# Gated hidden values kept in DRAM by tiles of tokens, one of their loads behind the keys and queries, and the last turn of maxima four slots later

## The chip, the cores and the metric

The kernel runs on one core of a Trainium2 chip. The metric is the device time of one execution in microseconds (us); the time before is the median of three runs.

## The reference, cut to what matters

`x` is [2, 1024, 512] in float32, that is 2048 tokens. The layer normalises it and feeds it to a causal attention with 32 heads of 16 (8 groups of keys and values, each for 4 heads) and to a gated feed-forward net; the input is added at the end.

```python
xn = layernorm(x)
q = (xn @ Wq)                      # 32 heads of 16
k, v = (xn @ Wkv)                  # 8 groups, each for 4 heads
w = softmax(where(causal, -inf, q @ k.T) / 4)
s = (w @ v) @ Wo + bo
gate = xn @ gate_w.T + (xn @ gate_a.T) @ gate_b.T
up = xn @ up_w.T + (xn @ up_a.T) @ up_b.T
hidden = silu(gate) * up           # [2048 tokens, 1376]
y = hidden @ down_w.T + (hidden @ down_a.T) @ down_b.T
out = x + s * silu(y)
```

## The kernel before

**Precision.** Matrix products of float32 values are done on high and low parts: three products (high by high, high by low, low by high) stand for one. So the gated values `hidden` exist twice, as `hid_hi` and `hid_lo`.

**Stages.** Tokens come in 4 chunks of 512 (`NCH`, `C`) or 16 tiles of 128 (`NT`, `P`), and the 1376 hidden values in 11 blocks `h` of at most 128 (`NH`). After some 100 us of normalising and projecting, two streams of work run side by side on every engine. The *attention* goes through 16 groups (`N`, 8 groups of 2 sequences) in rounds of 40 slots (`SLOTS`). The *background* first makes the gated values (`hidden(h, c)`, 44 pieces), then folds the down weights (`fold_down(h)`, 11 pieces), then does the down product of 16 tiles of tokens (`down(t)`) with the output product (`output(t)`) one tile behind, or four behind for the last tiles. `interleave` decides when background steps come between two slots; it counts steps and knows no times.

**The gated values in DRAM.** All 1376 hidden values of a tile are needed for its down product, but they are made block by block. So `store_hidden` writes each piece to the scratch tensor `hid`, laid out as [2 parts, 11 blocks, 128 rows, 2048 tokens]: a row of a piece is 512 tokens, 2048 bytes in one run. `load_hidden(t)` reads the 2 x 11 x 128 rows of a tile back, 128 tokens of each, 512 bytes in one run (2816 runs, 1408 KB), into one of two buffers `hin`, which the down product reads. Block 10 has only 96 rows, so SP writes zeros to its last 32 rows of `hid` at the start. Loads 0 and 1 stand in the order of SP behind the fold of block 5, load t + 2 behind the down product of tile t.

**SP issues every DMA**, in one order and on one hardware queue. Its attention part issues, for the group to come, keys and queries (`L867`, `L870`, slot 1 of a round) and values (`L878`, slot 19), and the attention output and its sums (`L894`, `L898`, `L902`). If SP waits, everything behind it waits too.

**Maxima.** The softmax needs the maximum of each row ahead. For each group TensorE (PE) makes the scores once in bank `s` (`L1146`) for VectorE (DVE) to take maxima (`L1723`, `L1726`); `split_max` (`L1733` to `L1739`) puts them into `neg_pad`. Then comes a *turn*: PE transposes `neg_pad` (`L1153`), ScalarE (ACT) copies it to `neg_rows` (`L1450`), and SP copies it in four small DMAs into two rows of `q` (`L886`), so that the second score product (`st`, `L1165`) has the maximum in it. That product runs a group behind the first one; the exponentials (`L1442`) and the product with the values (`o`, `L1182`) follow. Each group has two turns, one for each half of its rows. The second must have landed at slot 12 of the group's own round.

**What sets the place of a turn.** `STREAM` lists score units and turns; `stream_slots` gives each a slot. The second turn of a group stands behind the first pair of units of the next group, which is slot 6 of its own round. The very last turn has no next group: it stands in the slot of the last pair of units, slot 2 of round 15. Before a turn PE waits in `turn_max` for `m_split`, the end of `split_max`.

Of the kernel before, what the change touches and what calls it, by code (L numbers as in the profile page):

```python
# [6 lines left out]
F32 = mybir.dt.float32  # L7
# [6 lines left out]
P = 128  # L14
C = 512
# [3 lines left out]
B, T, D, F, R = 2, 1024, 512, 1376, 16  # L19
H, G = 32, 8  # L20
HD, REP = D // H, H // G
TOK = B * T
KT = D // P
NCH, TT = TOK // C, C // P
NT = TOK // P
NH = -(-F // P)
rows = [min(P, F - P * h) for h in range(NH)]
FULL = F // P
NBLK = H * HD // P + 1
N = B * G  # L30
QT = T // P
ROWS = 3 * HD
AUG = ROWS + 2
# [47 lines left out]

LOAD, LOAD_V = 1, 19
FIRST_UNIT, UNIT_SLOTS = 6, 39
FIRST_OF_ALL = 10

EVEN_SLOTS = range(22, 31)
# [54 lines left out]
def out_behind(t):  # L141


    if t >= NT - TT:
        return t - TT
    return t - 1 if 1 <= t <= NT // 2 else None
# [110 lines left out]
def stream_slots():  # L257

    weight = [150 + spec[2] for _, _, spec in UNIT]
    slots, slot = [], -1
    for kind, n in STREAM:
        if kind == "unit" and n % 2 == 0:
            g, w = divmod(n, NU)
            first = FIRST_UNIT if g else FIRST_OF_ALL
            even = SLOTS * g + first + (UNIT_SLOTS + FIRST_UNIT - first) * sum(weight[:w]) // sum(weight)
            even -= even % 2
            slot = max(even, slot + 1)
            if slot - SLOTS * g in EVEN_SLOTS:  # L270
                slot += slot % 2
        slots.append(slot)
    return slots


STREAM_SLOT = stream_slots()


# [11 lines left out]

def layer(nc, x, Wq, Wkv, Wo, bo, gate_w, up_w, down_w, low_a, low_b, low_a_down, low_b_down, out):
    scratch = dict(
        q=[B, H, AUG, T], k=[G, B, 3, HD, T], v=[G, B, P, QT, HD], hid=[2, NH, P, TOK],
        o=[B, 2, 2 * HD, H, C], r=[B, 2, H, C],
    )
    s = {n: nc.dram_tensor(f"scratch_{n}", shape, F32).ap() for n, shape in scratch.items()}
    with ExitStack() as ctx:

        def sbuf(stack, name, shape, dt=F32):
            return stack.enter_context(nc.sbuf_tensor(name, shape, dt))  # L300

        def in_place(stack, name, shape, part):


            with ExitStack() as brief:
                whole = sbuf(brief, name, shape)
            return whole, sbuf(stack, name + part, shape, F32R)
# [5 lines left out]
        q = sbuf(ctx, "q", [P, 2, 2, T], F32R)  # L313
        k = sbuf(ctx, "k", [P, 2, T], F32R)
        v = sbuf(ctx, "v", [P, 3, QT, 2, HD])
# [17 lines left out]
        with ExitStack() as first:  # L333
# [15 lines left out]
            with ExitStack() as own:  # L349
# [5 lines left out]
                hid, hid_l = in_place(own, "hid", [P, 2, C], "_lo")  # L355


        zeros = prob[:, 0, 0]
# [7 lines left out]
        with ExitStack() as second:  # L366
# [7 lines left out]
            late, hin = in_place(second, "late_context", [P, 2, 2, NH, P], "_hid_in")  # L374
# [116 lines left out]
        def wait_filled(engine, key):  # L491
            engine.wait_ge(filled, NUMBER[key] + 1)
# [49 lines left out]
        def _(pool):  # L542
# [44 lines left out]
            def low_context(t):  # L587
                pool.wait_ge(ch_done, CONTEXT_COUNT[t])
                _, whole, _, hi, lo = context_place(t)
                pool.tensor_tensor(lo, whole, hi, ALU.subtract).then_inc(cl_done, 1)  # L590
# [67 lines left out]
        def _(sp):  # L658
# [60 lines left out]
            def load_more_raw(n):  # L719
                if n + 8 < RAWS:  # L720
                    load_raw(n + 8)

            def store_hidden(n):
                h, c = divmod(n, NCH)
                sp.wait_ge(hid_lo, n + 1)
                for j, part_ in enumerate((hid_h, hid_l)):
                    sp.dma_start(s["hid"][j, h, 0:rows[h], c * C:(c + 1) * C], part_[0:rows[h], n % 2].bitcast(F32))\
                        .then_inc(hid_stored[n % 2], DMA)

            def load_hidden(t):  # L730
                if t >= 2:
                    wait_filled(sp, ("down", t - 2, 0))
                else:
                    sp.wait_ge(zero_stored, (B + 2) * DMA)
                    for i in range(2):
                        sp.wait_ge(hid_stored[i], 2 * DMA * NH * NCH // 2)
                sp.dma_start(hin[:, t % 2].rearrange("p j h n -> p (j h) n").bitcast(F32),
                             s["hid"][:, :, :, t * P:(t + 1) * P].rearrange("j h p n -> p (j h) n"))\
                    .then_inc(hin_landed[t % 2], DMA)

            def load_out(t):
# [17 lines left out]
            def load_again(t):  # L759
                if t >= 5:  # L760
                    sp.wait_ge(r3_done, t - 4)
                sp.dma_start(xt[:, t % 5], x_tiles[t]).then_inc(x_again[t % 5], DMA)

            def store_out(t):
                sp.wait_ge(r3_done, t + 1)
                sp.dma_start(out_tiles[t], ring[:, t % 8]).then_inc(out_stored[t % 8], DMA)

            def background():
# [41 lines left out]
                for h in range(NH):  # L810
                    yield STEPS["down_fold"]
                    load_more_raw(RAW_DOWN + h)
                    if h == 2:
                        sp.dma_start(wo[:, :, :], Wo.rearrange("(p k) n -> p k n", k=KT)).then_inc(wo_landed, DMA)
                        sp.dma_start(bias[:, :], bo.rearrange("(o n) -> o n", o=1).to_broadcast((P, D)))\
                            .then_inc(wo_landed, DMA)
                    if h == 3:
                        store_hidden(NCH * NH - 1)
                    if h == 5:
                        load_hidden(0)  # L820
                        load_hidden(1)
                yield STEPS["rest"]
                load_out(0)
                load_again(0)
                for t in range(NT):
                    yield LOAD_AT
                    if t + 1 < NT // 2:
                        load_out(t + 1)
                    for ahead in {11: (8,), 12: (9, 10)}.get(t, ()):
                        load_out(ahead)  # L830
                    if t + 1 < NT - 3:
                        load_again(t + 1)
                    yield STEPS["down"] - LOAD_AT
                    if t + 2 < NT:
                        load_hidden(t + 2)
                    if 2 <= t < 2 + NT // 2:
                        store_out(t - 2)
                    if t == NT - 1:
                        load_out(NT - 2)
                    if out_behind(t) is not None:  # L840
                        yield STEPS["out"]
                        for ahead in {12: (11,), 13: (12,), 14: (13, 15)}.get(t, ()):
                            load_out(ahead)
                        if t > NT - TT:
                            store_out(out_behind(t) - 1)
                            load_again(t)
# [70 lines left out]
                sp.dma_start(s["q"][b, :, ROWS:, :].rearrange("h r (a n) -> h (r a) n", n=C), zeros)\  # L917
                    .then_inc(zero_stored, DMA)
            for j in range(2):
                sp.dma_start(s["hid"][j, FULL, rows[-1]:].rearrange("p (a n) -> (p a) n", n=C), zeros)\  # L920
                    .then_inc(zero_stored, DMA)
            sp.wait_ge(const, 4)
            for a in range(2):
# [874 lines left out]
```

## Time and profile before

| | us |
|---|---|
| median of 3 runs | 944.62 |
| the three runs | 943.69, 944.62, 946.37 |
| the profiled execution | 946.66 |
| its span, first to last instruction | 944.9 |

In the span PE is busy for 896.9 us (95%), DVE for 583.7 us, ACT for 488.5 us and GpSimd for 314.7 us. All 142946 packets move 129.20 MB at a mean of 137 GB/s. The mean granted clock of TensorE is 0.984 of full speed (2.4 GHz). A row of a timeline gives start and length in us, engine, line, operation, tiles and count; what stands in brackets at its end is how long the engine had been idle before it, and what released it. SPq is SP's DMA issue; its length is the time that issuing takes, not the transfer.

### The profile page before, as it was taken

Reading aid. Unit: us, or ns where it says so; the run is one execution under the profiler, and the core shown is the slowest. Engines: PE = TensorE matmul, PEld = TensorE weight load, DVE = VectorE, ACT = ScalarE, POOL = GpSimd, SP = SyncE. Lnnn points to the kernel's source line nnn. Section 1 sums busy time; section 2 is a strip of 40 time slices with the busy share of each in tenths; the row PEclk is TensorE's granted clock in tenths of the full one; section 3 lists DMA queues with packets and bytes.
Section 4 is the critical chain, followed back from the end, with each engine's and each line's share of the span. In section 5 each row is a group of like instructions: output and inputs, shape, how many; then the busy total and the mean of one; then the engine's idle time right before and its main releaser. Section 6 shows DMA issues by size and latency. Waiting matters only on the chain.

```text
span 944.9 us, 21107 instructions
## 1 busy us (share of the span) xinstructions
PE 896.9 (95%) x8075; PEld 633.1 (67%) x8075; DVE 583.7 (62%) x1688; ACT 488.5 (52%) x990; POOL 314.7 (33%) x316
## 2 busy tenths in 40 slices
PE   3898999999999999999999999999889999999997
PEld 3765667676766666667676766554667777777885
DVE  7756666666666666665656565777666666650136
ACT  3522656565555656565656565656445454546211
POOL 4231235252525343525252434441121313121133
PEclk9978999999999999999999999998999999999999
DMA  9466343333333342424242434347565647415774
GB/s 290 165 193 192 92 129 97 122 97 114 108 115 110 97 130 83 137 71 148 58 138 84 126 99 121 100 142 204 155 183 156 171 124 194 137 53 171 205 216 142
DMA packets 142946, 129.20 MB, mean 137 GB/s; under 512 B 36176, under 2 KB 104368, under 8 KB 142624
## 3 DMA queue, kind: packets, MB, share of 16 engines
q1 hardware_dynamic: 142848, 127.87, 45.6%
q8 instruction: 65, 1.06, 0.5%
q14 instruction: 33, 0.27, 0.1%
HBM read 74.07 MB, written 53.22 MB: 135 GB/s over the span
## 4 chain that ended last, share of the span: by engine, by line
PE 88%; DVE 5%; DMA 3%; ACT 2%; issue 2%; SPq 1%; DVEq 0%
PE bank L1011 27%; PE o L1182 14%; PE bank L1045 12%; PE s L1146 10%; PE st L1165 8%; PE bank L286 4%; PE bank L287 4%; PE bank L288 4%; DMA ring<-in_L_attn_x 2%; PE bank L986 1%; PE bank L990 1%; DMA q<-scratch_q 1%; DVE junk L1723 1%; PE s L1153 1%; ACT prob L1442 1%
## 5 line engine op out<-in xcount | busy, mean ns | idle before, releaser
L1442 ACT ACTIVATE prob<-st 128x512 f32<-128x512 f32 (+1 forms) x640 | 323.2, 554 | 263.4 <-PE st L1165 262.8
L1723 DVE CUSTOM_DVE_ANT_0 junk<-s,mask 128x128 bf16<-128x128 f32 (+3 forms) x512 | 229.1, 487 | 69.7 <-PE s L1146 67.9
L1726 DVE TENSOR_REDUCE part_max<-s 128x1 f32<-128x512 f32 x256 | 164.0, 682 | 116.3 <-PE s L1146 116.1
L1146 PE MATMUL s<-k,q 64*128 64x512 f32 (+3 forms) x768 | 150.7, 379 | 12.2 <-DVE part_max L1723 4.6
L567 POOL TENSOR_SCALAR_AFFINE_SELECT prob<-prob 128x512 f32<-128x512 f32 x128 | 81.8, 652 | 225.8 <-ACT prob L1442 224.3
L1011 PE MATMUL bank<-x_hi,w_hi 64*128 64x512 f32 (+1 forms) x704 | 150.2, 412 | 2.4 <-DVE hid L1564 1.1
L1182 PE MATMUL o<-prob,v 128*32 128x512 f32 (+3 forms) x1536 | 145.4, 497 | 0.0
L1011 PE MATMUL bank<-x_lo,w_hi 64*128 64x512 f32 (+1 forms) x704 | 142.8, 391 | 0.0
L1011 PE MATMUL bank<-x_hi,w_lo 64*128 64x512 f32 (+1 forms) x704 | 142.1, 389 | 0.0
L1165 PE MATMUL st<-q,k 64*128 64x512 f32 (+3 forms) x768 | 130.7, 356 | 2.3 <-ACT prob L1442 1.8
L1146 PEld LDWEIGHTS s<-k,q 64*128 64x128 f32 x768 | 79.1, 188 | 53.6 <-DVE part_max L1723 24.4
L1045 PE MATMUL bank<-down_hi,late_context_hid_in 64*128 64x256 f32 x1056 | 113.7, 288 | 0.3 <-DVE y L1580 0.3
L576 POOL TENSOR_TENSOR tanh<-tanh,hid 128x512 f32<-128x512 f32 (+1 forms) x44 | 56.6, 1286 | 163.7 <-DVE hid L1564 163.7
L1045 PEld LDWEIGHTS bank<-down_hi,late_context_hid_in 64*128 64x128 f32 x1056 | 91.4, 189 | 17.9 <-issue 16.9
L1011 PEld LDWEIGHTS bank<-x_hi,w_hi 64*128 64x128 f32 (+1 forms) x704 | 69.4, 182 | 40.1 <-issue 30.6
L1165 PEld LDWEIGHTS st<-q,k 64*128 64x128 f32 x768 | 73.5, 186 | 28.5 <-issue 11.0
L1182 PEld LDWEIGHTS o<-prob,v 128*32 128x32 f32 x1536 | 39.7, 110 | 64.0 <-issue 58.1
L584 POOL TENSOR_TENSOR hid_lo<-hid,tanh_hid_hi 128x512 fp32r<-128x512 f32 (+1 forms) x44 | 56.8, 1292 | 71.8 <-ACT tanh_hid_hi L1299 71.8
L1045 PE MATMUL bank<-down_lo,late_context_hid_in 64*128 64x256 f32 x528 | 77.5, 281 | 0.9 <-issue 0.9
L1011 PEld LDWEIGHTS bank<-x_lo,w_hi 64*128 64x128 f32 (+1 forms) x704 | 69.2, 182 | 12.3
L1011 PEld LDWEIGHTS bank<-x_hi,w_lo 64*128 64x128 f32 (+1 forms) x704 | 69.4, 183 | 7.7
L578 POOL TENSOR_TENSOR hid<-tanh,hid 128x512 f32<-128x512 f32 (+1 forms) x44 | 56.7, 1288 | 3.5
(148 smaller groups left out, 1089.0 us busy)
## 6 DMA issues: line engine op xcount, KB each, us to landing
late_context_hid_in<-scratch_hid SPq DMA_DIRECT2D x16, 1408.0 KB, 7.2
q<-scratch_q SPq DMA_DIRECT2D x60, 200.0 KB
scratch_hid<-tanh_hid_hi SPq DMA_DIRECT2D x40, 256.0 KB, 2.1
scratch_hid<-hid_lo SPq DMA_DIRECT2D x40, 256.0 KB, 2.4
scratch_o<-o_sb SPq DMA_DIRECT2D x32, 256.0 KB
scratch_q<-proj_hi SPq DMA_DIRECT2D x30, 256.0 KB
k<-scratch_k SPq DMA_DIRECT2D x30, 192.0 KB
x_again<-in_L_attn_x SPq DMA_DIRECT2D x16, 256.0 KB, 4.4
```

The lines of the kernel that those rows point to most:

```text
L567: ins = pool.affine_select(out=blk, in_=blk, compare_op=ALU.is_ge, fill=0.0, base=0, pattern=[[0, REP], [1, P]], channel_multiplier=-1)
L576: pool.tensor_tensor(th[0:hp, n % 2], th[0:hp, n % 2], hid[0:hp, n % 2], ALU.mult).then_inc(tanh_used, 1)
L578: pool.tensor_tensor(hid[0:hp, n % 2], th[0:hp, n % 2], hid[0:hp, n % 2], ALU.add).then_inc(hid_done, 1)
L584: pool.tensor_tensor(hid_l[0:hp, n % 2], hid[0:hp, n % 2], hid_h[0:hp, n % 2], ALU.subtract)\
L1011: mm = pe.matmul(bank[i][0:hp, :], w_[half, h % 2, i, kt, 0:hp], x_[half, c, kt], start=not cross and kt == 0 and w_ is wh and x_ is xh, s ...
L1045: mm = pe.matmul(bank[i][:, COLUMNS[i]], lhs[half], rhs[half, COLUMNS[i]], start=not cross and n == 0 and m == 0, stop=cross == 1 and n == ...
L1146: pe.matmul(sb_[(p + odd) % S_BANKS][:, 0:wd], q[half, g % 2, h // 2, qt * P:(qt + 1) * P], k[half, g % 2, k0:k0 + wd], start=True, stop=T ...
L1165: mm = pe.matmul(st[odd][:, col:col + q1 - q0], k[half, i % 2, kt * P:(kt + 1) * P], q[half, i % 2, h // 2, q0:q1], start=True, stop=True)
L1182: mm = pe.matmul(ob[32 * h:32 * h + 2 * HD, q0 % C:q0 % C + q1 - q0], v[:, i % 3, kt].rearrange("p a e -> p (a e)"), prob[:, job % 3, h, c ...
L1442: nc.scalar.activation(prob[:, job % 3, h, 0:JOB_COLS[j]], st[at % ST_BANKS][:, 0:JOB_COLS[j]], ACT.Exp, scale=float(HD) ** -0.5).then_inc ...
L1723: ins = dve.tensor_tensor_reduce(junk[:, n % S_BANKS, 0:wd], bank_[:, 0:wd], mask[:, C - wd:C], 1.0, LOWEST, ALU.add, ALU.max, part[:, h, ...
L1726: ins = dve.tensor_reduce(part[:, h, qt, dst:dst + 1], bank_[:, 0:wd], AX.X, ALU.max)
```

## The change

There are four parts.

1. `hid` is laid out as [16 tiles, 128 rows, 2 parts, 11 blocks, 128 tokens]. A load of a tile now reads 128 runs of 11264 bytes, where it read 2816 of 512 bytes. A store of a piece now writes 4 runs of 512 bytes for each row, where it wrote one of 2048 (512 runs for 128). The two zero fills write 512 runs of 512 bytes each, from 128 rows of 2048. The bytes are the same.
2. Load 0 stands behind the fold of block 4, load 1 behind that of block 6.
3. Load 2 stands five steps into `down(1)`, behind the keys and queries of the next group; it stood behind `down(0)`, ahead of them.
4. The last turn is four slots later, in slot 6 of round 15.

```diff
--- before.py
+++ after.py
@@ -81,6 +81,7 @@
 
 LOAD, LOAD_V = 1, 19
 FIRST_UNIT, UNIT_SLOTS = 6, 39
+LAST_TURN = 4
 FIRST_OF_ALL = 10
 
 EVEN_SLOTS = range(22, 31)
@@ -270,6 +271,8 @@
             if slot - SLOTS * g in EVEN_SLOTS:
                 slot += slot % 2
         slots.append(slot)
+
+    slots[-1] += LAST_TURN
     return slots
 
 
@@ -290,7 +293,7 @@
 
 def layer(nc, x, Wq, Wkv, Wo, bo, gate_w, up_w, down_w, low_a, low_b, low_a_down, low_b_down, out):
     scratch = dict(
-        q=[B, H, AUG, T], k=[G, B, 3, HD, T], v=[G, B, P, QT, HD], hid=[2, NH, P, TOK],
+        q=[B, H, AUG, T], k=[G, B, 3, HD, T], v=[G, B, P, QT, HD], hid=[NT, P, 2, NH, P],
         o=[B, 2, 2 * HD, H, C], r=[B, 2, H, C],
     )
     s = {n: nc.dram_tensor(f"scratch_{n}", shape, F32).ap() for n, shape in scratch.items()}
@@ -724,7 +727,8 @@
                 h, c = divmod(n, NCH)
                 sp.wait_ge(hid_lo, n + 1)
                 for j, part_ in enumerate((hid_h, hid_l)):
-                    sp.dma_start(s["hid"][j, h, 0:rows[h], c * C:(c + 1) * C], part_[0:rows[h], n % 2].bitcast(F32))\
+                    sp.dma_start(s["hid"][TT * c:TT * (c + 1), 0:rows[h], j, h].rearrange("t p n -> p t n"),
+                                 part_[0:rows[h], n % 2].bitcast(F32).rearrange("p (t n) -> p t n", t=TT))\
                         .then_inc(hid_stored[n % 2], DMA)
 
             def load_hidden(t):
@@ -734,8 +738,8 @@
                     sp.wait_ge(zero_stored, (B + 2) * DMA)
                     for i in range(2):
                         sp.wait_ge(hid_stored[i], 2 * DMA * NH * NCH // 2)
-                sp.dma_start(hin[:, t % 2].rearrange("p j h n -> p (j h) n").bitcast(F32),
-                             s["hid"][:, :, :, t * P:(t + 1) * P].rearrange("j h p n -> p (j h) n"))\
+                sp.dma_start(hin[:, t % 2].rearrange("p j h n -> p (j h n)").bitcast(F32),
+                             s["hid"][t].rearrange("p j h n -> p (j h n)"))\
                     .then_inc(hin_landed[t % 2], DMA)
 
             def load_out(t):
@@ -816,8 +820,9 @@
                             .then_inc(wo_landed, DMA)
                     if h == 3:
                         store_hidden(NCH * NH - 1)
-                    if h == 5:
+                    if h == 4:
                         load_hidden(0)
+                    if h == 6:
                         load_hidden(1)
                 yield STEPS["rest"]
                 load_out(0)
@@ -830,8 +835,10 @@
                         load_out(ahead)
                     if t + 1 < NT - 3:
                         load_again(t + 1)
+                    if t == 1:
+                        load_hidden(2)
                     yield STEPS["down"] - LOAD_AT
-                    if t + 2 < NT:
+                    if 1 <= t < NT - 2:
                         load_hidden(t + 2)
                     if 2 <= t < 2 + NT // 2:
                         store_out(t - 2)
@@ -917,7 +924,7 @@
                 sp.dma_start(s["q"][b, :, ROWS:, :].rearrange("h r (a n) -> h (r a) n", n=C), zeros)\
                     .then_inc(zero_stored, DMA)
             for j in range(2):
-                sp.dma_start(s["hid"][j, FULL, rows[-1]:].rearrange("p (a n) -> (p a) n", n=C), zeros)\
+                sp.dma_start(s["hid"][:, rows[-1]:, j, FULL], zeros)\
                     .then_inc(zero_stored, DMA)
             sp.wait_ge(const, 4)
             for a in range(2):
```

SP around the start of the down products. L737 of before and L741 of after are the load of a tile of hidden values, L867/L874 and L870/L877 the next keys and queries. Before:

```order
L727 DMA scratch_hid<-hid_lo 96x512
L737 DMA late_context_hid_in<-scratch_hid 128x22x128 x2
L894 DMA scratch_o<-o_sb 4x32x512
...
L762 DMA x_again<-in_L_attn_x 128x512
L737 DMA late_context_hid_in<-scratch_hid 128x22x128
L867 DMA k<-scratch_k 48x1024 x2
L870 DMA q<-scratch_q 50x1024 x4
L754 DMA ctx<-scratch_o 128x4x128
L756 DMA inv_sums<-scratch_r 128x4x128
L762 DMA x_again<-in_L_attn_x 128x512
L894 DMA scratch_o<-o_sb 4x32x512
```

After:

```order
L730 DMA scratch_hid<-hid_lo 96x4x128
L741 DMA late_context_hid_in<-scratch_hid 128x2816
L901 DMA scratch_o<-o_sb 4x32x512
...
L766 DMA x_again<-in_L_attn_x 128x512
L874 DMA k<-scratch_k 48x1024 x2
L877 DMA q<-scratch_q 50x1024 x4
L758 DMA ctx<-scratch_o 128x4x128
L760 DMA inv_sums<-scratch_r 128x4x128
L766 DMA x_again<-in_L_attn_x 128x512
L741 DMA late_context_hid_in<-scratch_hid 128x2816
L901 DMA scratch_o<-o_sb 4x32x512
```

Load 2 went from ahead of the keys and queries to a place five DMAs and more behind them; the second of the first two loads stands two DMAs further back.

PE at the last turn (`neg_pad` to `s`). Before:

```order
L1165 MATMUL st<-q,k 128x512 x2
L1146 MATMUL s<-k,q 128x512 x2
L1153 MATMUL s<-ident,neg_pad 32x128
L1182 MATMUL o<-prob,v 32x256 x4
L1045 MATMUL bank<-wo_hi,ctx_hi 128x256 x2
```

After, four slots on:

```order
L1172 MATMUL st<-q,k 128x384 x2
L1172 MATMUL st<-q,k 128x128 x2
L1160 MATMUL s<-ident,neg_pad 32x128
L1189 MATMUL o<-prob,v 32x512 x4
L1052 MATMUL bank<-down_hi,late_context_hid_in 128x256 x2
```

The turn now stands behind two more second score products of round 15 and an output product; nothing else changed its place on PE.

SP at the same time of the program, before:

```order
L762 DMA x_again<-in_L_attn_x 128x512
L886 DMA q<-neg_rows 2x4x128 x4
L737 DMA late_context_hid_in<-scratch_hid 128x22x128
L766 DMA out<-ring 128x512
L894 DMA scratch_o<-o_sb 4x32x512
L898 DMA sums<-scratch_o 128x16
```

After:

```order
L766 DMA x_again<-in_L_attn_x 128x512
L741 DMA late_context_hid_in<-scratch_hid 128x2816
L770 DMA out<-ring 128x512
L901 DMA scratch_o<-o_sb 4x32x512
L893 DMA q<-neg_rows 2x4x128 x4
L905 DMA sums<-scratch_o 128x16
```

The four small DMAs of the turn now stand behind a hidden load, a store of results and a store of attention output.

## Rows read from the trace of the kernel before

**Rows 1.** Page, part 1: busy us (share of the span) x instructions.
```profile
PE 896.9 (95%) x8075; PEld 633.1 (67%) x8075; DVE 583.7 (62%) x1688; ACT 488.5 (52%) x990; POOL 314.7 (33%) x316
```
**Rows 2.** Busy us (x instructions) of PE, PEld, DVE, ACT, POOL; clock; DMA share; GB/s.
```profile
100.00:600.00 500.00, 498.32 (x4258) 336.44 (x4256) 319.74 (x984) 294.72 (x604) 207.49 (x205) 1.00 0.36 109
```
**Rows 3.** What PE waited for in 640 to 945: us, times, longest.
```profile
PE s L1146 <- DMA q<-scratch_q: 2.1, 1, 2.1
PE s L1153 <- DVE neg_pad L1739: 2.0, 1, 2.0
```
**Rows 4.** Timeline of SP, from load 2 to the turn behind it.
```profile
680.72 0.38 SPq L737 DMA_DIRECT2D late_context_hid_in<-scratch_hid  x1
681.21 3.50 SPq L867 DMA_DIRECT2D k<-scratch_k  x2
684.75 1.48 SPq L870 DMA_DIRECT2D q<-scratch_q  x4
...
694.06 2.64 SPq L886 DMA_DIRECT2D q<-neg_rows  x4
```
**Rows 5.** Timeline of PE across the wait for the queries.
```profile
690.34 0.50 PE L1165 MATMUL st<-q,k 64*128 64x384 f32 x4
692.93 0.47 PE L1146 MATMUL s<-k,q 64*128 64x128 f32 x2 [2.08 <-DMA q<-scratch_q]
...
697.52 0.28 PE L1165 MATMUL st<-q,k 64*128 64x256 f32 x2
```
**Rows 6.** Windows for PE behind both long waits: busy, clock, DMA share, GB/s.
```profile
693.00:694.00 1.00, 1.00 (x7) 0.50 0.64 156
...
843.00:844.00 1.00, 0.46 (x6) 1.00 0.00 0
```
**Rows 7.** Timeline of PE, the same stretch of the next round.
```profile
744.55 0.27 PE L1146 MATMUL s<-k,q 64*128 64x128 f32 x2
...
747.61 0.28 PE L1165 MATMUL st<-q,k 64*128 64x256 f32 x2
```
**Rows 8.** Timeline of SP, keys and queries of that next round.
```profile
734.32 0.81 SPq L867 DMA_DIRECT2D k<-scratch_k  x2
735.17 1.48 SPq L870 DMA_DIRECT2D q<-scratch_q  x4
```
**Rows 9.** Timeline of PE, last turn to slot 12 of round 15.
```profile
843.54 0.28 PE L1153 MATMUL s<-ident,neg_pad 128*32 128x128 f32 x1 [2.04 <-DVE neg_pad L1739]
...
847.92 1.06 PE L1182 MATMUL o<-prob,v 128*32 128x512 f32 x8
...
853.19 0.43 PE L1165 MATMUL st<-q,k 64*128 64x512 f32 x2
```
**Rows 10.** Timeline of SP at the last turn.
```profile
844.15 2.58 SPq L886 DMA_DIRECT2D q<-neg_rows  x4
```
**Rows 11.** A turn in the hidden stage: SP, then PE's slot 12.
```profile
587.78 2.68 SPq L886 DMA_DIRECT2D q<-neg_rows  x4
...
593.30 0.42 PE L1165 MATMUL st<-q,k 64*128 64x512 f32 x2
```
**Rows 12.** What SP waited for in 110 to 600.
```profile
SPq L886 <- ACT neg_rows L1450: 90.2, 20, 6.8
```
**Rows 13.** Small DMA of 8 KB (tile sums), issue to landing.
```profile
DMA to landing us min/median/max: 1.5/2.1/7.2
```
**Rows 14.** Windows for PE: runs of 2 KB and more; runs of 512 bytes.
```profile
8.00:12.00 4.00, 0.00 (x0) 1.00 1.06 384
...
660.00:664.00 4.00, 3.01 (x27) 1.00 1.15 342
```
**Rows 15.** Chain in order of time: the load of x at the start.
```profile
16.11 9.91 DMA ring<-in_L_attn_x
```
**Rows 16.** Timeline of SP: behind 1024 runs of 512 bytes, and behind few.
```profile
726.67 1.41 SPq L762 DMA_DIRECT2D x_again<-in_L_attn_x  x1
...
826.26 0.43 SPq L762 DMA_DIRECT2D x_again<-in_L_attn_x  x1
```

## Prediction, made before the changed kernel ran

> **What bounds the kernel now.** The page's busy times come first: PE is busy for 896.9 of 944.9 us, every other engine for 62% or less [rows 1]. Nothing is won by making another engine faster; what counts is where PE stands still or runs at half clock. The stretches say where: from 100 to 600 PE is busy for 498.32 of 500 us at full clock [rows 2], so the ten rounds of hidden values have 1.7 us to give in all, and only something that makes PE wait can change them. What is lost lies at the start and behind 600. There the list of PE's waits names two long ones that single places cause: 2.1 us for the queries and 2.0 us for `neg_pad` [rows 3]. The timelines of PE and SP at these two places carry the rest.
>
> The sum goes against the profiled execution, 946.66 us. That is 2.04 us above the median of 944.62; I take the difference to be spread that the change leaves alone, and take the same sum off the median.
>
> **Load 2 behind the keys and queries.** SP issues the load of a hidden tile at 680.72 in 0.38 us, and then needs 3.50 us for the two key DMAs, which took 0.81 us one round later [rows 4, 8]. So the issue itself was held for 2.7 us, with 2816 runs of the load still outstanding. The queries come out at 684.75 instead of about 682, and their data stand behind the load in the same queue. PE needs them at 690.84 and gets them at 692.93: 2.08 us idle [rows 5]. In the next round, with no load just ahead, the keys are issued at 734.32 and PE uses them at 744.55 with no wait, 10.2 us later [rows 7, 8]. In the changed kernel the keys come out at 681.2 (SP waits there for a score product that is done by then), 9.6 us before 690.84. What must move in front of them is gone: the load took 1408 KB, at 297 GB/s (below) 4.9 us of the queue, plus the 2.7 us of held issue. Together 7.6 us earlier against 2.08 us of wait leaves 5.5 us to spare. This term is **-2.08**.
>
> The clock goes with it. Behind the gap the granted clock falls to 0.50, that is from 2.4 to 1.2 GHz [rows 6]. From the first score of that slot to the second score product of slot 8 PE takes 697.52 - 692.93 = 4.59 us; the same work one round later takes 747.61 - 744.55 = 3.06 us [rows 5, 7]. The half clock costs 1.53 us. PE was dense before the gap, so without the gap I expect no fall: **-1.53**. The bounds are 0 (the fall comes anyway) and -1.53.
>
> What is late next: load 2 itself is not, since it comes out at about 685.5 and `down(2)` starts a whole tile later. The turn behind it (at 694.06 [rows 4]) moves up by the gap too, to about 691.8 to 694.4, and its data stand behind queries, context and load 2. Slot 12 of that round is then near 699: 690.84 plus 8.2 us (the 9.8 us it takes now less 1.53). A turn's last DMA may be late there by 0 to 0.5 us; I take 0, because the whole queue has nearly drained by 697 in the trace of before with the same bytes.
>
> **The last turn.** PE waits 2.04 us for the end of `split_max` [rows 9]. Four slots later, at 847.92 - 2.04 = 845.9, `neg_pad` is long done: **-2.04**, with no clock to win, as the clock stayed at 1.00 there [rows 6]. But the turn has a reader: slot 12, at 853.19 - 2.04 = 851.15 [rows 9]. PE's turn ends at 846.15, the copy by ACT behind an exponential at 846.8, SP issues four DMAs in about 2.6 us [rows 10] to 849.5. The smallest DMAs take 2.1 us from issue to landing [rows 13], of which 0.46 is issue, so the last lands at about 851.1. From the other side: in the hidden stage the issue ends at 590.46 and PE goes on at 593.30 without a wait [rows 11], so 2.84 us are surely enough, which would be 852.35. The new wait is between 0 (that median, empty queue) and 1.2 us; I take **+0.5**, nearer to the small DMA's own duration. On SP the four DMAs now stand behind hidden load, result store and output store. These three can go out from 841.1, when their waits are met, and 1.9 MB take under 6 us, so the queue is empty before 849; if it is not, each us of backlog is a us at slot 12.
>
> **The layout, loads.** Rows of 11264 bytes instead of 512. With long rows (x, weights, mostly 2 KB and more) the queue moved 384 GB/s at a share of 1.06, that is 362 at full share; with rows of 512 bytes 342 at 1.15, that is 297 [rows 14]. A load of 1408 KB thus needs 4.0 us of the queue instead of 4.9, and with 128 runs instead of 2816 SP should no longer be held for about 3 us behind each of 16 loads. PE waits for none of the other loads or for what follows them (no other DMA is among its waits), so this is **0**, with cover by PE's own work. Bounds 0 and about -0.5, if the wait of a later stage hangs on it by a chain I don't see.
>
> **The layout, stores.** 88 stores write four times the runs. At 297 instead of 362 GB/s each takes 0.16 us longer; the DMA share in that stage is 0.36 [rows 2], and the buffer is used again two pieces (20 us) later. **0** as long as SP keeps its slack: see the third rival. The zero fills are another matter. They stand ahead of the third load of x at the start, and the chain goes through that load for 9.91 us [rows 15] at a full queue. Half a MB costs 1.77 us at 297 and 1.45 at 362: **+0.3**, bounds 0 and 0.6.
>
> By the Trainium skill (DMA: Bandwidth & Descriptors, the table at its head) 512 bytes are already enough for line rate. Then the zero fills would cost nothing and the sum would be -5.2 instead of -4.9; the two windows above speak for a fifth less, though what else ran in them differs.
>
> **The first two loads.** SP waits at load 0 until the last store of hidden values has landed, before and after, so moving it up one block changes nothing; load 1 behind two small DMAs leaves room for them. PE's waits from 655 to 680 are for DVE and ACT. **0**.
>
> **Sum:** -2.08 - 1.53 - 2.04 + 0.5 + 0.3 = **-4.85 us**: 941.8 against the profiled execution, **939.8** against the median.
>
> **Rivals.**
>
> *The gain is half of that (941.3 to 943.0).* The turn's landing takes the place of one of the two waits: +1.2 at slot 12 of round 15, or a like wait in the first round of down products, or the clock falls in spite of the gap being gone. For it: the path at round 15 has no spare time at all in my own working, and the half clock hangs on one gap of 2.08 us, while one of 2.04 us at 841.5 left the clock at 1.00 [rows 6]. Against it: other turns never make PE wait. With one of these the sum is -3.3, with all three -1.6.
>
> *Ten engines.* By the Trainium skill (DMA: Bandwidth & Descriptors, why a DMA increments its semaphore by 16) a DMA whose outer dimension is 50 runs on ten of the sixteen engines, and the queries have 50 rows. The mechanism in rows: while only queries were left the DMA share was 0.64 [rows 6], ten sixteenths. Four queries of 200 KB then take 800 KB / (10/16 x 362 GB/s) = 3.6 us on these engines. If the queries are the long pole by themselves, they wait on even with load 2 behind them; but keys and queries together would be there within 2 + 1.1 + 3.6 = 6.7 us of 681.2, at about 688, still 2.8 us early. With this the q wait would stay only if another 2.8 us stood ahead: then only the last turn gains, -1.2, 943.4.
>
> *Slower, 948 to 951.* Each pair of stores leaves 1024 runs of 512 bytes in the queue. Behind as many (context and inverse sums) SP took 1.41 us for a DMA that otherwise takes 0.43 [rows 16]. If stores hold SP like that, the turns of the eleven rounds of hidden values go out late, and each round may lose 1 us on a PE that has none to spare: +11 - 4.85 = +6. Against it: SP waited 90.2 us before 20 of the turns of that stage, 4.5 us each [rows 12]; only a delay of more than that, or one that falls between the copy and the last DMA, reaches PE. This decides it: SP late by over 4.5 us at a turn.
>
> *More (936.5 to 938).* The other stretches at half clock (near 645 and 666) hang on small gaps; a shift of the schedule can clear one.
>
> **How the numbers follow.** Forecast 0.60, half gain 0.20, queries still late 0.05, slower 0.07, more 0.08. The predicted time is that of the forecast, 939.8. The range of 8 in 10 runs from 936.8 (part of the last case) to 943.8, which takes in the half gain and late queries. About 0.3% of the time, 2.8 us, is what a measurement of this kernel tells from no change, so faster means below 941.8: nearly all of the forecast and of the case above it, and a little of the half gain, 0.69. Same (941.8 to 947.5) is 0.24, slower 0.07.
>
> **What would show it.** Right: no wait of PE on `q` near 690, full clock from 690 to 700, no wait of PE for `neg_pad`, keys issued near 681.3 in about 0.8 us, result stores behind hidden loads in about 0.5 us instead of over 3, some 9,200 packets fewer (16 x 2688 = 43,008 fewer in the loads, 80 x 384 + 8 x 288 = 33,024 more in the stores, 768 more in the zero fills), and the 100 to 600 stretch again above 498 us busy. Wrong: an idle time of PE before a `st` at slot 12 (behind 698 or near 851), stores followed by issue times above 1 us and PE waits in the hidden stage, or a start that is later than before by over 0.6 us at the first hidden product.

## The result, and the profile after

| | before | after |
|---|---|---|
| median of 20 runs, us | 945.96 | 938.97 |
| lowest and highest | 941.38, 950.45 | 934.72, 944.88 |
| profiled execution | 946.66 | 940.22 |
| its span | 944.9 | 938.5 |

The ratio is 0.9931 [0.9913, 0.9949]: 6.5 us faster, between 4.8 and 8.2. A second series of the changed kernel gave 0.9942 [0.9915, 0.9968]. The median lies 0.8 us below the forecast of 939.8 and inside its range. That it lies so close is in part luck: the forecast started from 944.62, and over 20 runs the kernel before has 945.96, from which the same sum gives 941.1. The gain is larger than the 4.85 us of the sum, which stands at the very edge of the interval.

The busy times and the stretch of the hidden values, the same views as [rows 1] and [rows 2]:

```profile
PE 894.9 (95%) x8075; PEld 632.1 (67%) x8075; DVE 582.7 (62%) x1688; ACT 488.3 (52%) x990; POOL 314.7 (34%) x316
DMA packets 133730, 129.20 MB, mean 138 GB/s; under 512 B 36176, under 2 KB 104368, under 8 KB 131360
```
```profile
100.00:600.00 500.00, 498.29 (x4260) 335.74 (x4258) 320.56 (x985) 295.43 (x605) 206.84 (x204) 1.00 0.39 108
```

PE is busy for 498.29 us of that stretch (498.32 before): the stores of 512-byte runs cost it 0.03 us, which is nothing. There are 9,216 packets fewer, as counted ahead.

What PE waits for from 640 on, with us, times and longest, in place of [rows 3]:

```profile
PE s L1153 <- DVE part_max L1730: 1.9, 5, 0.8
...
PE st L1172 <- DMA q<-neg_rows: 0.2, 1, 0.2
```

Neither the queries nor `neg_pad` are in the list any more; a wait of 0.2 us for the landing of the last turn is new. One more wait is gone that nobody had forecast. In the kernel before PE stood still for 0.88 us in the middle of a down product, and the profile shows nothing that it waited for:

```profile
808.65 0.28 PE L1045 MATMUL bank<-down_lo,late_context_hid_in 64*128 64x256 f32 x1 [0.88 <-issue]
```

SP around load 2 (L741) and its keys (L874) and queries (L877), in place of [rows 4]:

```profile
681.14 0.80 SPq L874 DMA_DIRECT2D k<-scratch_k  x2
681.99 1.48 SPq L877 DMA_DIRECT2D q<-scratch_q  x4
...
685.51 0.43 SPq L741 DMA_DIRECT2D late_context_hid_in<-scratch_hid  x1
688.75 0.60 SPq L901 DMA_DIRECT2D scratch_o<-o_sb  x1
691.91 2.66 SPq L893 DMA_DIRECT2D q<-neg_rows  x4
```

The keys take 0.80 us where they took 3.50, and the whole group is out 2.8 us earlier. PE then goes through the place of [rows 5] without stopping and with a full clock (the window's columns are length, busy of PE, PEld, DVE, ACT, POOL, granted clock, DMA share, GB/s):

```profile
690.60 0.50 PE L1172 MATMUL st<-q,k 64*128 64x384 f32 x4
690.94 0.27 PE L1153 MATMUL s<-k,q 64*128 64x128 f32 x2
...
694.00 0.28 PE L1172 MATMUL st<-q,k 64*128 64x256 f32 x2
```
```profile
690.00:691.00 1.00, 1.00 (x17) 0.79 (x14) 0.40 (x2) 0.55 (x2) 0.19 (x1) 1.00 1.28 276
```

From the first score to the second score product of slot 8 it takes 694.00 - 690.94 = 3.06 us, to the digit what the next round took before [rows 7].

The last turn on PE, in place of [rows 9], and SP beside it, in place of [rows 10]:

```profile
840.93 0.28 PE L1160 MATMUL s<-ident,neg_pad 128*32 128x128 f32 x1
...
846.81 0.50 PE L1172 MATMUL st<-q,k 64*128 64x512 f32 x2 [0.23 <-DMA q<-neg_rows]
```
```profile
836.39 0.32 SPq L741 DMA_DIRECT2D late_context_hid_in<-scratch_hid  x1
836.76 0.43 SPq L770 DMA_DIRECT2D out<-ring  x1
838.28 0.57 SPq L901 DMA_DIRECT2D scratch_o<-o_sb  x1
841.81 2.59 SPq L893 DMA_DIRECT2D q<-neg_rows  x4
```

Along the program the changed kernel stands ahead by 1.0 us at the second turn (98.08 for 99.13), by nothing at 659 (659.52 for 659.37), by 2.2 at 691, 3.5 at 711, 4.7 at 811 and 6.4 at the end (times of the changed kernel). The steps at 691 and 711 are the wait for the queries and the half clock behind it, the step up to 811 is for the most part the 0.88 us in the down product, and the last one is the turn. The 1.0 us that comes and goes again goes with the clock: before 100 the old kernel had some 17 us at half clock and the new one 13.6, and around 645 it was 6.8 and 10.2 us.

### The profile page after: what moved, and what is told of

It is laid out like the page before. It is cut to its first block, busy times and chain, and to the rows that moved or that the text cites. A ratio compares the mean times of both kernels' runs of the same rounds, so it can differ in the third digit from the quotient of the medians.

```text
span 938.5 us, 21107 instructions
## 1 busy us (share of the span) xinstructions
PE 894.9 (95%) x8075; PEld 632.1 (67%) x8075; DVE 582.7 (62%) x1688; ACT 488.3 (52%) x990; POOL 314.7 (34%) x316
## 4 chain that ended last, share of the span: by engine, by line
PE 88%; DVE 4%; ACT 2%; SPq 2%; issue 2%; DMA 2%; DVEq 0%; ACTq 0%
PE bank L1018 27%; PE o L1189 15%; PE bank L1052 12%; PE s L1153 10%; PE st L1172 8%; PE bank L289 4%; PE bank L290 4%; PE bank L291 4%; PE bank L993 1%; DMA ring<-in_L_attn_x 1%; PE bank L997 1%; ACT prob L1449 1%; SPq L933 1%; PE s L1160 1%; DVE junk L1730 1%
```

## The experiments

Every ratio is against the kernel before, run in turn with it. The last two columns are means over the runs: the span, and the time at half clock, worked out as 2 x (1 - mean granted clock) x span. The first row has the 69 runs of the kernel before that ran beside the experiments; for the 20 of the result no spans and clocks are on record. The differences of the last two columns are therefore not pairs, and the ratio is the better measure of a gain.

| kernel | ratio [95%] | runs | span | half clock |
|---|---|---|---|---|
| before, beside the experiments | | 69 | 942.95 | 30.4 |
| only the turn | 0.9974 [0.9951, 0.9996] | 12 | 939.80 | 27.3 |
| only the order of loads | 0.9979 [0.9960, 0.9997] | 12 | 940.36 | 28.8 |
| only the layout | 1.0002 [0.9988, 1.0016] | 12 | 942.62 | 29.1 |
| all but the turn | 0.9975 [0.9958, 0.9992] | 12 | 939.87 | 28.4 |
| turn two slots later | 0.9923 [0.9899, 0.9948] | 11 | 936.04 | 24.3 |
| turn eight slots later | 0.9983 [0.9957, 1.0009] | 12 | 941.57 | 30.0 |
| stores twice | 0.9956 [0.9927, 0.9985] | 10 | 939.34 | 28.0 |
| the changed kernel, both series | 0.9931 and 0.9942 | 32 | 937.43 | 26.5 |

**Only the turn.** The kernel before, with the last turn in slot 6.

```diff
+LAST_TURN = 4
...
+    slots[-1] += LAST_TURN
```

> The kernel before with the last turn four slots later and nothing else. Theory (the sum of the prediction holds term by term): the 2.04 us wait for neg_pad goes, and 0.2 to 0.5 us of waiting for the landing of neg_rows takes its place at slot 12 of round 15, so 1.5 to 1.8 us less than before. The wait for the queries near 690 stays at 2.1 us. Rival (the gain came from something else, the turn is worth nothing because slot 12 then waits as long): within 0.5 us of before, with an idle time of about 2 us at slot 12.

The wait for `neg_pad` is gone, the one for queries stays, and the landing of the turn is waited for:

```profile
688.93 0.33 PE L1148 MATMUL s<-k,q 64*128 64x128 f32 x2 [1.73 <-DMA q<-scratch_q]
```
```profile
846.44 0.50 PE L1167 MATMUL st<-q,k 64*128 64x512 f32 x2 [0.50 <-DMA q<-neg_rows]
```
```profile
836.16 3.13 SPq L768 DMA_DIRECT2D out<-ring  x1
839.34 0.57 SPq L896 DMA_DIRECT2D scratch_o<-o_sb  x1
841.16 2.59 SPq L888 DMA_DIRECT2D q<-neg_rows  x4
```

The store of results is held for 3.13 us behind a load in the old layout (0.43 in the new one, above). SP is free again at 839.9, ahead of the turn, so that holding by itself costs nothing here. The landing costs 0.5 us, and the edit gains about 2.5 us by the ratio, where I had expected 1.5 to 1.8; the interval, 0.4 to 4.6 us, takes in both.

**Only the order of loads.** Old layout, old turn, loads 0 to 2 as in the changed kernel.

```diff
-                    if h == 5:
+                    if h == 4:
                         load_hidden(0)
+                    if h == 6:
                         load_hidden(1)
...
+                    if t == 1:
+                        load_hidden(2)
...
-                    if t + 2 < NT:
+                    if 1 <= t < NT - 2:
```

> The kernel before with the old layout of hid, loads 0 and 1 split over the folds of blocks 4 and 6, and load 2 behind the keys and queries. Theory: the order alone is enough, PE does not wait for the queries and keeps full clock from 690 to 700, 3.4 to 3.6 us less than before; SP is still held for about 3 us behind each load. Rival (the layout did it): the wait for the queries stays near 2 us.

The wait for queries is gone, but another has come eight microseconds later, that for the turn of this round:

```profile
684.03 0.43 SPq L737 DMA_DIRECT2D late_context_hid_in<-scratch_hid  x1
687.07 5.03 SPq L897 DMA_DIRECT2D scratch_o<-o_sb  x1
692.14 2.82 SPq L889 DMA_DIRECT2D q<-neg_rows  x4
```
```profile
698.34 0.50 PE L1168 MATMUL st<-q,k 64*128 64x512 f32 x2 [0.69 <-DMA q<-neg_rows]
```

The load's 2816 runs now hold the store of attention output for 5.03 us, until 692.10, and the turn, which PE made at 689.45 and ACT had copied by 690.2, goes out only then. In the changed kernel this store takes 0.60 us (688.75, above) and slot 12 waits for nothing. It is the one place where the held issue was seen to reach PE, and the layout removes it. The edit gains 2.0 us by the ratio (0.3 to 3.8), where I had expected 3.4 to 3.6.

**Only the layout.** New layout, old order of loads, old turn.

```diff
-        q=[B, H, AUG, T], k=[G, B, 3, HD, T], v=[G, B, P, QT, HD], hid=[2, NH, P, TOK],
+        q=[B, H, AUG, T], k=[G, B, 3, HD, T], v=[G, B, P, QT, HD], hid=[NT, P, 2, NH, P],
...
-                sp.dma_start(hin[:, t % 2].rearrange("p j h n -> p (j h) n").bitcast(F32),
-                             s["hid"][:, :, :, t * P:(t + 1) * P].rearrange("j h p n -> p (j h) n"))\
+                sp.dma_start(hin[:, t % 2].rearrange("p j h n -> p (j h n)").bitcast(F32),
+                             s["hid"][t].rearrange("p j h n -> p (j h n)"))\
...
```

> The new layout with the old order of loads and the old place of the turn. Theory (the queries were late by held issue and by the bytes in front of them): the keys come out 2.7 us earlier and the 1408 KB ahead of them move about 0.9 us faster, 3.6 us together against a wait of 2.1 us, so the wait is gone here too, about 3.5 us less than before, less up to 0.3 us for the zero fills. Rival (only the bytes ahead count, not the held issue): 1.2 us of waiting and the half clock stay, at most 1 us less than before.

```profile
679.22 0.33 SPq L741 DMA_DIRECT2D late_context_hid_in<-scratch_hid  x1
679.65 1.38 SPq L871 DMA_DIRECT2D k<-scratch_k  x2
681.07 1.64 SPq L874 DMA_DIRECT2D q<-scratch_q  x4
```
```profile
690.65 0.33 PE L1150 MATMUL s<-k,q 64*128 64x128 f32 x2 [1.33 <-DMA q<-scratch_q]
```

This refuted my theory. The queries' issue begins 1.85 us behind the load's, where it was 4.03 in [rows 4], and the wait is there all the same. In the old layout PE gets its queries 12.2 us after the load's issue (692.93 - 680.72), in the new one 11.4 (690.65 - 679.22); it wants them 10.1 us after it in both. And even the difference of 0.8 isn't safe: over four profiles with the old layout and the old order it is 11.4 to 12.2 us (11.4 in the second profile of the kernel before, below). So here the queries were not late by the time that SP was held: their issue moved up by 2.2 us and their arrival by 0 to 0.8. The rival that I had written beside the theory, only the bytes ahead count, gave a wait of 1.2 us, and 1.33 was measured.

**All but the turn.** The changed kernel with its last turn in slot 2.

```diff
-LAST_TURN = 4
+LAST_TURN = 0
```

> The changed kernel without its last part: new layout, new order, last turn in its old slot. Theory (layout and order remove the same wait, so they do not add): 3 to 3.6 us less than before, equal to the order alone and to the layout alone, and 1.8 us more than the changed kernel. Rival (the layout has a gain of its own beside it): at least 1 us less than the order alone.

Neither queries nor the first round's turn are waited for. The wait for `neg_pad` is back, and this time PE works on at 1.2 GHz behind it (columns from here on: length, PE busy, granted clock, DMA share, GB/s):

```profile
837.02 0.28 PE L1160 MATMUL s<-ident,neg_pad 128*32 128x128 f32 x1 [2.04 <-DVE neg_pad L1746]
```
```profile
839.00:840.00 1.00, 1.00 (x14) 0.50 0.01 4
```

With that the order and the layout together are worth about what the order is alone, 2.4 and 2.0 us by the ratios (I had expected 3 to 3.6 for both), and the turn on top of them brings the rest.

**The turn at other slots.** The changed kernel with two and with eight slots instead of four.

```diff
-LAST_TURN = 4
+LAST_TURN = 2
```

> The changed kernel with the last turn two slots later instead of four. Theory: slot 4 of round 15 begins about 0.3 us after neg_pad is done, so PE waits for nothing there, and the four small DMAs go out 1.7 us earlier, so the 0.23 us of waiting at slot 12 goes too: 0 to 0.3 us less than the changed kernel. Rival (neg_pad is not done by then): a wait before the turn of up to 0.5 us, no gain.

> The changed kernel with the last turn eight slots later (slot 10 of round 15). Measures the path from a turn to slot 12 by itself. Theory: copy, four issues of 0.65 us and a landing take 5.5 us from the turn on; slot 12 is 1.2 us behind slot 10, so PE waits about 4 us there, and the clock may fall behind it (1.5 us): 3.5 to 6 us more than the changed kernel. Rival (the landing takes only as long as the last issue): 3 us more.

With two slots PE waits for neither end of the turn:

```profile
836.42 0.28 PE L1160 MATMUL s<-ident,neg_pad 128*32 128x128 f32 x1
...
843.77 0.43 PE L1172 MATMUL st<-q,k 64*128 64x512 f32 x2
```

With eight, slot 12 comes too soon:

```profile
841.38 0.28 PE L1160 MATMUL s<-ident,neg_pad 128*32 128x128 f32 x1
845.85 0.50 PE L1172 MATMUL st<-q,k 64*128 64x512 f32 x2 [2.91 <-DMA q<-neg_rows]
```
```profile
842.05 2.59 SPq L893 DMA_DIRECT2D q<-neg_rows  x4
```
```profile
848.00:849.00 1.00, 1.00 (x10) 0.50 0.00 0
```

The kernel with eight slots and the changed kernel give the length of a turn. From its start on PE to the data it is 845.85 - 841.38 = 4.47 us when the queue is empty, and in the changed kernel 846.81 - 840.93 = 5.88 us, with a load and two stores ahead in the queue. They take it to a share of 1.01 at 840 and 0.81 at 841. The load has landed at 842.85 and the result store at 843.53; then the share stays at 0.25 to 0.27 until 845.5 and is gone by 846, and the turn's data come at 846.81. So the tail of the store of attention output is what still stands beside the turn at its end. I had expected a wait of about 4 us with eight slots, from a turn of 5.5 us; it is 2.91, and the turn takes 4.47. By the ratios this kernel is some 3.9 us slower than the changed one, as expected (3.5 to 6). Two slots give the lowest median of all kernels here, 937.26 us. Against four slots that is not a measured gain: the intervals of their ratios overlap almost wholly.

**Stores twice.** The changed kernel with every store of hidden values made a second time, into a copy that nobody reads.

```diff
+                    for where in ("copy", "hid"):
+                        sp.dma_start(s[where][TT * c:TT * (c + 1), 0:rows[h], j, h].rearrange("t p n -> p t n"),
...
```

> The changed kernel with every store of gated values issued twice, the first time into a spare tensor: 22 MB and 33,000 runs of 512 bytes more, 88 more issues on SP. Theory (SP and queue have slack in the hidden stage): PE busy from 100 to 600 stays above 497.5 us, time within 1.5 us of the changed kernel, the last store before load 0 perhaps 1 us later and hidden. Rival (the third rival of the prediction: stores hold SP and make turns late): at least 5 us more, with PE waits for neg_rows or queries in the hidden stage.

```profile
315.51 0.40 SPq L731 DMA_DIRECT2D scratch_copy<-tanh_hid_hi  x1
315.94 0.51 SPq L731 DMA_DIRECT2D scratch_hid<-tanh_hid_hi  x1
316.50 0.57 SPq L731 DMA_DIRECT2D scratch_copy<-hid_lo  x1
317.11 0.56 SPq L731 DMA_DIRECT2D scratch_hid<-hid_lo  x1
```
```profile
100.00:600.00 500.00, 497.44 (x4247) 1.00 0.53 150
```

SP needs 0.4 to 0.6 us for nearly every store, twice as many or not (the longest took 2.51 here), and PE loses 0.85 us in 500, a little more than I had allowed (497.5 busy). What it waits for there is DVE's `hid`, twice, 0.9 us in all, and no turn. The ratio, 0.9956 [0.9927, 0.9985], can't be told from that of the changed kernel. The rival in which the stores hold SP and the kernel gets slower is refuted for this kernel, with a factor of two to spare.

**Once more the changed kernel.**

> The changed kernel on the chip of this call, as the reference for the three others. Theory: 4.5 to 7 us less than before, of which 5.2 to 5.5 us are the two waits and the half clock, and the rest comes and goes with where half-clock stretches fall in the first 100 us and near 645.

The median is 939.48 against 945.17, 5.5 us less by the ratio and as expected, the profile has a span of 934.4 us and no wait for `neg_rows` of 0.15 us or more: the 0.23 us of the first profile come and go.

**Once more the kernel before, and the kernel before half a microsecond later.**

```diff
+            sp.wait_ge(zero_made, 1)
```

> The kernel before once more, for a second profile of it. Both theories: median ratio 1. Open is what the TensorE clock does behind the two waits of about 2 us. If a fall behind such a wait is a matter of the execution, the two half-clock stretches (behind the queries at 690 and behind the maxima at 841) come and go: the wait for queries, seen three times with a fall, should again show 2.0 us and 0.50 behind it, the wait for maxima, seen with a fall in two profiles of four, is open at even odds. If the fall there is tied to the code, this profile shows 1.00 behind the maxima again, as the first one of this kernel did.

> The kernel before with one thing moved: the start's x loads are issued after the zero fills have finished, some 0.5 us later, so that everything behind comes by about that much later. The computation is the whole one. Again open is the clock behind the two waits of 2 us: if it is the phase of the execution that decides, the stretches at 1.2 GHz stand elsewhere than in the kernel before, and their sum lies anywhere between 20 and 32 us as in the profiles so far; the span goes with that sum at half its size, so 941 to 946 us. If they are tied to the code, they stand where the kernel before has them and the span is 945.4.

Each of the two is a single execution, for its profile alone. The second profile of the kernel before has both waits, and the clock behaves in the opposite way: full behind the queries, half behind the maxima.

```profile
678.28 0.38 SPq L737 DMA_DIRECT2D late_context_hid_in<-scratch_hid  x1
```
```profile
689.67 0.33 PE L1146 MATMUL s<-k,q 64*128 64x128 f32 x2 [1.29 <-DMA q<-scratch_q]
```
```profile
690.00:691.00 1.00, 1.00 (x10) 1.00 0.61 178
...
839.00:840.00 1.00, 1.00 (x12) 0.50 0.00 0
```

I had expected the fall behind the queries in any case; that half of the expectation missed. The shifted kernel waited 1.79 and 2.04 us, and its clock fell behind both; its profile has a span of 945.7 us with 37.8 us at half clock, more than the 20 to 32 that I had expected. Over the profiles with these waits the clock fell behind the queries in four of five, and behind `neg_pad` in four of six. At these two places the fall belongs to the execution and not to the place in the code. That is not so everywhere: a wait of 1.25 us for DVE's `part_max` near 664 is followed by a stretch at half clock in all twelve profiles.

Both profiles also show the idle time in the down product again, 0.63 us at 803.30 and 1.17 us at 807.82. So it is there in all three profiles of the kernel before and its shifted copy, and in none of the other nine, the three with a single part of the change among them. What it is stays open: its releaser is unseen, and since it is gone with the turn alone, with the order alone and with the layout alone, it can't be put down to any one of them.

## Why the prediction came out right, step by step

**The wait for queries, -2.08.** Right in cause: the load ahead of them was the cause, and taking it away ended the wait. The size is right for the compared profile, but it is the longest of four: with the old layout and order PE waited 2.08, 1.79, 1.73 and 1.29 us, 1.7 in the mean. Wrong in the working. "Together 7.6 us earlier against 2.08 us of wait leaves 5.5 us to spare" counted the held issue of 2.7 us as a delay beside the 4.9 us of the queue. The run with the layout alone shows that it isn't one. From it the queries arrive 11.4 us behind the load's issue, of which the load in the new layout is some 4.0 (an estimate of the prediction): 7.4 us, or 7.0 from the keys' issue, which begins 0.43 us later. PE wants them at 690.94 - 681.14 = 9.8. To spare are then 2.8 us, an estimate. The sign was safe, the margin half of what I wrote.

**The half clock behind it, -1.53.** Right for the two profiles that I compared, 3.06 us for 4.59. As an expectation over many runs it was too large: the kernel before doesn't pay it in every execution.

**The last turn, -2.04, "with no clock to win".** The wait is gone, as forecast. The clock at 1.00 in one profile [rows 6] was taken for a property of the place. In four profiles of six it falls there, and then costs as much as behind the queries: from the turn to slot 12 PE takes 11.1 to 11.2 us in these four and 9.65 in the other two. As an expectation over many runs this is the term that was wrong, by about 1.0 us (four sixths of 1.5, an estimate), and it was put at nothing from one profile.

**What the sum left out.** In the two compared profiles the clock behind `neg_pad` had no part, as it stood at 1.00 there before. Their spans differ by 6.4 us, and the sum gave 4.85. The difference is the idle time of 0.88 us in the down product, which the sum didn't know, 0.27 us less at the landing, 0.15 us less at the zero fills and 0.2 of small ones: 2.08 + 1.53 + (2.04 - 0.23) + 0.88 = 6.3. The row was in the trace of before (a wait of 0.9 us by `issue`) and was passed over; no run shows whether the change removed it or another effect did.

Over all runs the clock's part can be worked out. The mean span falls from 942.95 (standard error 0.30) to 937.43 (0.47): 5.5 us. Time at half clock falls from 30.4 (0.8) to 26.5 us (1.1). Across all 182 of these runs, within each kernel, a microsecond at half clock goes with 0.32 us of span; where PE is the bound throughout it would be 0.50. So 1.2 to 1.9 us of the 5.5 came by the clock and 3.6 to 4.3 from waits and the rest, an estimate: the 3.9 us less at half clock have a standard error of 1.4 themselves. The sum had 1.53 for the clock and 3.32 for the rest. Against 5.5 us the sum isn't clearly short. That the rest of the way to the 6.5 us of the paired ratio is luck of the 20 runs fits its interval, and isn't shown.

**The landing of the last turn, +0.5.** 0.23 and under 0.15 us in two profiles, 0.28 with the stores doubled, 0.50 with the old layout. The end of the bound at 1.2 was never reached. The turn took longer than I had it (5.9 us instead of 5.2, by "the last lands at about 851.1" from a turn at 845.9), since the queue wasn't empty; slot 12 came 5.65 us behind the turn instead of the 5.25 that I had reckoned, which gave it more room.

**The turn behind load 2, 0.** Right for the changed kernel, and it hung on the layout: with the order alone it was 0.69 us. I took 0 from a queue that drains by 697; the actual cause was SP, held for 5.03 us.

**Layout.** Loads and stores 0, together with the zero fills 1.0002 [0.9988, 1.0016]. The load of a tile lands in 6.5 us instead of 7.2 (medians of 16), which is near the 0.9 us that the two windows [rows 14] gave, and nothing waits for it. By the Trainium skill (DMA: Bandwidth & Descriptors, the table at its head) 512 bytes reach line rate, and the two numbers should be alike; here the long runs are a tenth faster from issue to landing. The zero fills seem to cost 0.15 us instead of 0.3: the load of x in the chain now ends at 26.17, and ended at 26.02 before [rows 15]. But over all profiles that load lands at 25.2 to 26.0 with the old layout and at 25.2 to 26.5 with the new one, so a cost of this size isn't shown.

```profile
17.79 8.38 DMA ring<-in_L_attn_x
```

**The first two loads, 0.** No wait came of them in any profile; their part was not run apart from that of load 2.

**The rivals.** *Half of the gain*: none of its three conditions struck the changed kernel. The wait in the first round exists, 0.69 us with the order alone. The landing at its bound of 1.2 us was never seen, and behind the gap that is gone the clock stayed full from 690 to 700 in all seven profiles with the new order. The arithmetic of the case was loose too: with the landing at 1.2 alone the sum is -4.15, and -3.3 only where the clock falls. *Ten engines*: not decided, and its reading of [rows 6] was wrong. At 693 not only queries were left: the context, inverse sums and `x` issued from 686.27 on landed at 694.94, 697.12 and 697.76, and the share was 0.67 and 0.65 in the next two microseconds as well. Its 3.6 us are for four queries, but PE's first score waits for the keys and the first two only. The case asked for the wait to stay in the changed kernel, and it is gone; no run changed the number of rows. *Slower*: refuted by the doubled stores. *More*: the other stretches at half clock moved about (before 100, near 645, 666 and 940), but in every kernel, and with no tie to the change that these runs show.

**A better version.** The turn two slots later instead of four has no wait at either end. That is the profile's answer; a gain in time over four slots isn't measured. What PE still waits for behind 640 are 0.2 to 1.3 us at a time for DVE and ACT, and once 1.6 us with no releaser in the profile.

## What to carry to other kernels

A wait of PE should be costed as the wait plus a share of the half clock behind it, and how often the clock falls has to be asked of several executions: one profile says full or half, and here its answer held as a rule at neither place. A DMA that SP issues late because an issue ahead was held need not be late by that time: here 2.2 us earlier on SP brought the data 0 to 0.8 us earlier, with the same bytes ahead. What did suffer was something small and urgent, a turn of maxima, that stood behind the held instruction. A hand-off between two engines over DMA has two ends to be late at, so the place to look for is the one where neither waits: here it took 4.5 us with an empty queue and 5.9 us with a load and two stores ahead. And a gain that comes out larger than the sum has to be accounted for along the program before it is put down to luck or to the clock: here 0.9 us of it was an idle time that stood in the trace from the start.

## What the runs showed of the hardware

Issue time on SP depends on the runs of the DMAs ahead. A result store issued right behind a load of 2816 runs of 512 bytes held SP for 3.1 to 5.2 us; right behind the same bytes in 128 runs of 11264 bytes it took 0.4 to 1.8 us, 0.43 in most cases. It isn't so behind every load: behind the fourth, at 699.99 in the kernel before, the store of attention output took 0.57 us in either layout. With the new layout single issues further back still took up to 3.0 us. The time until the data of the queries arrived was nearly the same (11.4 to 12.2 us behind the load's issue, and 11.4).

The TensorE clock fell from 2.4 to 1.2 GHz behind 9 of the 12 waits of 1.3 to 2.9 us for queries, `neg_pad` and `neg_rows` in these profiles, and at the same wait of the same program in one execution and not in another. Behind the wait of 1.25 us near 664 it fell in all twelve. The time at half clock per execution went from 9 to 44 us over 69 runs of the one kernel before; by the 0.3 us of span for each such us this is most of its spread of 938 to 951 us, and larger than the change that was to be measured.
